# Stacking the keys and queries of the first batch pair by pair, with the expert loads behind, and two experts split early by GpSimd in place of three

## The reference, cut to what matters

```
x  = x + tanh(g_xattn) * (attention(layernorm(x), ctx) @ Wo + bo)
x  = x + tanh(g_ffn)   * moe(layernorm(x))
```

## Time and profile before

| | |
|---|---|
| median of 3 runs | 173.44 us (171.92 to 175.43) |
| the profiled execution | 172.02 us, of which its span 169.7 us |
| busy: PE, DVE, POOL, ACT | 139.7, 131.2, 126.8, 109.6 us |
| transfers | 13.99 MB, mean 82 GB/s |

### The profile page before, as it was taken

How to read it: one execution, slowest core, us unless ns; L and a number is a source line. 1 busy time by engine, 2 the same in 40 slices (tenths; PEclk the granted TensorE clock), 3 DMA queues, 4 the chain that set the end, 5 groups by cost and what they waited for, 6 DMA issues and landing times.

```text
span 169.7 us, 4332 instructions
## 1 busy us (share of the span) xinstructions
PE 139.7 (82%) x1724; PEld 111.5 (66%) x1724; DVE 131.2 (77%) x255; ACT 109.6 (65%) x182; POOL 126.8 (75%) x90
## 2 busy tenths in 40 slices
PE   7789588558699989999998892979866995999953
PEld 4435234335478768787787792869856994999952
DVE  1779999667667868768869689989999889454691
ACT  3369583329969979899968998569523462555600
POOL 7609999919999999989777955596557585868750
PEclk9999999999999999999999999999996999999999
DMA  4598699990004800995000000340000000100000
GB/s 136 184 315 211 196 238 242 220 251 14 6 0 85 198 1 16 217 233 191 4 4 0 4 0 0 108 144 6 2 0 0 4 0 4 31 0 4 0 0 31
DMA packets 12925, 13.99 MB, mean 82 GB/s; under 512 B 1470, under 2 KB 9579, under 8 KB 12907
## 3 DMA queue, kind: packets, MB, share of 16 engines
q1 hardware_dynamic: 12906, 13.73, 30.4%
HBM read 7.18 MB, written 0.26 MB: 44 GB/s over the span
## 4 chain that ended last, share of the span: by engine, by line
PE 32%; DVE 28%; POOL 10%; ACT 9%; DMA 8%; SPq 6%; issue 5%; DVEq 0%; ACTq 0%
PE banks L906 5%; DVE kab L852 5%; PE banks L908 5%; PE banks L907 5%; POOL kab L549 4%; ACT kab L642 4%; DVE v_lo L720 3%; DMA kab<-k_nat 3%; DVE nmax L735 3%; PE banks L1006 3%; PE banks L1007 3%; PE banks L987 3%; DMA ring<-in_L_ffn_w_dram 3%; SPq L425 2%; DVE gtop L763 2%
## 5 line engine op out<-in xcount | busy, mean ns | idle before, releaser
L549 POOL TENSOR_TENSOR kab<-kab 128x1024 f16<-128x1024 f32 (+1 forms) x18 | 41.1, 2283 | 17.3 <-DVE kab L852 17.3
L521 POOL TENSOR_TENSOR p_lo<-prob,p_hi 128x768 f16<-128x768 f32 x31 | 50.3, 1642 | 3.1 <-ACT p_hi L606 2.6
L642 ACT ACTIVATE kab<-banks,b1T 128x256 f32<-128x256 f32 x72 | 28.2, 478 | 24.3 <-PE banks L908 15.9
L735 DVE TENSOR_REDUCE nmax<-banks 128x1 f32<-128x768 f32 x32 | 30.5, 954 | 12.5 <-PE banks L988 12.5
L598 ACT ACTIVATE prob<-banks 128x768 f32<-128x768 f32 x32 | 25.8, 805 | 9.1 <-PE banks L1007 8.1
L906 PE MATMUL banks<-wf,kab 128*128 128x128 f16 x144 | 26.2, 224 | 5.8 <-POOL kab L549 4.5
L606 ACT ACTIVATE p_hi<-prob 128x768 f16<-128x768 f32 x32 | 27.0, 843 | 1.0
L852 DVE CAST kab<-kab 128x1024 f16<-128x1024 f32 (+1 forms) x19 | 19.5, 1031 | 9.8 <-ACT kab L642 9.8
L908 PE MATMUL banks<-wf,kab 128*128 128x128 f16 x144 | 26.2, 224 | 0.0
L907 PE MATMUL banks<-wf,kab 128*128 128x128 f16 x144 | 26.2, 224 | 0.0
L1006 PE MATMUL banks<-qab,kab 128*128 128x256 f16 x96 | 23.0, 273 | 0.7 <-DVE qab L832 0.7
(11 more groups left out here) (144 smaller groups left out, 340.3 us busy)
## 6 DMA issues: line engine op xcount, KB each, us to landing
ring<-in_L_ffn_w_dram SPq DMA_DIRECT2D x16, 256.0 KB, 4.1
kab<-k_nat SPq DMA_DIRECT2D x4, 384.0 KB, 4.4
kab<-k_nat SPq DMA_DIRECT2D x6, 192.0 KB, 4.4
kab<-k_nat SPq DMA_DIRECT2D x2, 576.0 KB, 7.2
qab<-qo SPq DMA_DIRECT2D x2, 384.0 KB, 6.2
kab<-k_nat SPq DMA_DIRECT2D x2, 288.0 KB, 7.8
prob<-in_ctx_dram SPq DMA_DIRECT2D x2, 256.0 KB, 5.4
ring<-in_L_xattn_Wk_dram SPq DMA_DIRECT2D x2, 256.0 KB, 3.9
```

Source lines behind the costliest of these rows:

```text
L521: nc.gpsimd.tensor_tensor(p_lo[:, j % 3, dst, :], prob(j, g)[:, 0:n, :], p_hi[:, j % 3, dst, :], ALU.subtract).then_inc(pl_done, 1)
L549: nc.gpsimd.tensor_tensor(hid_lo[:, k % HB, cols], hid[:, k % 2, cols], hid_hi[:, k % HB, cols], ALU.subtract).then_inc(hl_done, 1)
L642: nc.scalar.activation(hid[:, k % 2, c * T1:(c + 1) * T1], span(2 * (k % 2), HC * T1)[:, c * T1:(c + 1) * T1], ACT.Gelu, bias=b1T[:, e * H ...
L735: nc.vector.tensor_reduce(nmax[:, i, q:q + 1], span(0, KEYS), AX_X, ALU.max, negate=True).then_inc(max_done, 1)
```

## The change

`GROUPS[0]` has four groups of one pair each in place of two groups, so the keys and queries of batch 0 go out in 32 transfers in place of 16, with the same bytes. `LOAD_AFTER` puts the load of expert 1 behind pair 2 (it was behind pair 0), and the loads of 2 and 3 behind pair 3 as before. `EARLY` is 2 in place of 3: expert 2 is split by ACT and DVE in steps 17 and 18 and no longer by GpSimd, and GpSimd splits `Wo` ahead of expert 1 in place of between 1 and 2.

```diff
@@ -63,7 +63,7 @@
 BIAS_STEP = 10
-EARLY = 3
+EARLY = 2
 FSPLIT0 = 15
@@ -130,7 +130,8 @@
-GROUPS = [[(0, 1), (1, PAIRS)], [(0, 2), (2, PAIRS)]]
+GROUPS = [[(p, p + 1) for p in range(PAIRS)], [(0, 2), (2, PAIRS)]]
+LOAD_AFTER = {2: [1], 3: [2, 3]}
@@ -434,9 +435,8 @@
             for n, (p0, p1) in enumerate(GROUPS[0]):
                 stack_k(0, p0, p1)
                 stack_q(p0, p1)
-                load_f(1 + n)
-            for j in range(1 + len(GROUPS[0]), RING):
-                load_f(j)
+                for j in LOAD_AFTER.get(n, []):
+                    load_f(j)
```

## The result

| | before | changed |
|---|---|---|
| median of 20 runs each | 172.8 us | 173.47 us |
| profiled execution, span | 172.02, 169.7 us | 173.3, 171.5 us |
| mean granted clock of PE | 0.988 | 0.959 |

The ratio is 1.0089, with a 95% interval of 1.006 to 1.0119: 1.5 us slower, where 0.85 us faster was forecast. The ratio leaves out the runs in which either kernel was over 1.5% slower than its fastest, so it can't be read off the two medians. The time lies in the stated range and within 2% of before, but on the wrong side of it.

A forecast was written before the change was run, and what follows sets the result against it. PE paces the heads, with its idle ahead of 47 us to gain. +0.2 - 2.0 + 0.95 = -0.85 us gives a median of 172.6 us; own range 171.5 to 173.6, 8-in-10 range 169.9 to 175.2 us.

The forecast's parts named there:

- Landing of pair 3's keys: Ahead of head 2: keys land at 35.5 us, ACT, DVE and PE wait behind them; +0.2 us.
- Half clock behind the one long idle: PE ahead of 38.3 us: idle of about 3.8 us; half clock no term of the sum, only a rival at 0.15.
- three short idles: PE up to head 2: waits of 1.72, 1.70 and 0.39 us become one of about 3.8 us; +0.2 us.
- GpSimd's -2.0 us: Heads: PE's two waits for GpSimd's lo parts, 0.93 and 1.08 us, both go; -2.0 us.
- rival 2: PE falls to half clock behind the idle ahead of 38.3 us, losing 1.7 us: 174.3 us; chance 0.15.
- ACT's split, +0.95 us: ACT's split of expert 2 right before the gelu table load, hidden by nothing: +0.95 us.
- Rival 1: Ahead of head 2: pair 3's keys land late, 175.1 us at a landing of 38 us; chance 0.2.
- Rival 3: Faster: keys land at 34.5 us, half-clock slice at 127 to 131 us spared; 169.9 us with both; chance 0.2.
- Loads 4 to 8: Expert loads in SP's queue: load 6 waits for DVE's split in step 18, nothing is delayed; 0.
- Batch 1 keys, forecast 0: Stacks of batch 1 stand ahead of load 4 and move with the heads; 0.

The follow-up runs named there:

- the filled idle: Changed kernel with 28 products of zeros in PE's idle ahead of the second maxima of head 2; ratio 1.0017 against the kernel before.
- both long idles filled: Changed kernel with products of zeros in PE's idles, 28 ahead of head 2's second maxima and 30 ahead of the gates' transposes; ratio 0.9954 against the kernel before.

## Why the prediction was wrong

**Landing of pair 3's keys: right.** 35.7 us for 35.5, and ACT, DVE and PE behind it in the order given; +0.40 us for +0.2. SP was 0.57 us late at the load of expert 1, 0.4 us of it by one held issue (1.03 us at 27.38 us), and the landing came 6.5 us behind the load's first issue in place of 6.9. That the load in front decides it was half right: with the load moved away it landed only 0.3 us earlier, and SP's issuing is the main part.

**Half clock behind the one long idle, at nothing in the sum: this is the step that failed.** The forecast hands three short idles to one of 3.8 us for +0.2 us, and lets GpSimd's -2.0 us arrive in full behind it; half clock is rival 2 at 0.15 and no term of the sum. The idle came, 3.59 us, and half clock with it: +1.16 us in the step behind it (zero with the idle filled), and +0.29 us up to head 5, with ACT kept waiting 2.69 us in that step. GpSimd's two waits went, but 1.45 us of the gain were given back this way. Shown by the filled idle and by `EARLY` = 2 alone, where 1.86 of the 2.01 us arrive. With both long idles filled the kernel is 0.8 us faster than before, which is the forecast's sum within its interval. Rival 2 had the mechanism and nearly the price, 1.7 us. That the median lies even in the forecast's own 171.5 to 173.6 us is luck: they were reckoned from a median of 173.44 us of three runs, and twenty gave 172.8 us.

**ACT's split, +0.95 us: right**, +0.94 us measured and 1.2 us gained by moving it. What I left out is its consequence: PE's wait for the gates grew from 3.04 to 3.99 us, and half clock followed in each execution whose wait was 3.99 us and unfilled; the rest of the changed kernel took 0.3 us more than with the wait filled. I had the 3.04 us row in front of me as a case without half clock and did not ask what 0.95 us more would do. That it is the length alone is not shown: behind a wait of 2.46 us, with the split moved, the clock fell too.

**Rival 1, late keys,** did not happen: every engine stood behind the keys as it says, but they landed 0.2 us behind the forecast, and the 32 transfers in place of 16 did not make the sum this rival's. **Rival 3** did not happen: the dip near 130 us stayed. **Loads 4 to 8:** the load of expert 6 was issued at 102.86 us and nothing waited for it, as forecast.

**Batch 1 keys, forecast 0:** +0.5 us. Of the executions profiled, PE's waits for them sum to 0.80 to 0.84 us in the four with two groups in batch 0, and to 0.82 to 1.50 us in the ten with pairs; the same kernel has 0.87 and 1.13 us, and with only fillings added to the changed kernel it was 0.94 and 1.50 us. What is more is mostly a second wait of 0.18 to 0.55 us, which five of the ten have and none of the four. So it may belong to the pairs; no run separates it, and its cause is open.

Sum of the forecast, corrected by the traces: +0.40 (landing) - 2.01 + 0.15 (GpSimd) + 1.16 + 0.29 (half clock) + 0.50 (batch 1 keys, open) + 0.94 (ACT's split) + 0.37 (behind it) are the 1.8 us of span. Of the last term 0.3 us go with the filled wait.

## What to carry to other kernels

Several short idles of the busiest engine and one long idle of the same sum are not the same: here TensorE went to half clock behind the long one, and the work behind it was the next to be late. When transfers are cut into pieces to have the first ones sooner, look for who waits for the last one, and what stands behind that waiter in its queue; here an engine's reuse of a buffer took the gain, for batch 1 keys that stood ahead of the first exponential in ACT's list and were not stacked before 52 us, and ordering the keys ahead of the queries that nobody needed yet gave it back. Moving ACT's item itself behind the first exponentials was not tried. Work taken over by another engine costs its full duration if it stands right before an unhidden table load; a dozen instructions earlier it was free.

## What the runs showed of the hardware

- Behind a longer idle ahead of head 2 the step from its second maxima to those of head 3 was longer: 3.58 or 3.59 us with idles up to 0.95 us, 4.06 us with 3.24, 4.74 us with 3.59, 5.31 and 5.30 us with 4.42 and 5.65. The clock could fall when PE was already at work again: 1.2 us behind the end of the idle of 3.24 us, 1 us behind one of 2.46 us.
- Half clock did not follow the length of an idle alone. Behind those four idles, and behind each unfilled 3.99 us ahead of the gates, the granted clock fell; behind 3.04 and 3.05 us there it did not, in two kernels, and behind 2.46 us, in three, it did (0.69 to 0.78 in the lowest stretch of 4 us, 0.57 in the third kernel), in two of them with the rest of the kernel no longer for it (69.3 to 69.6 us). Behind 2.81 or 2.82 us near 128 us it fell in five executions and did not in seven. From the transposes of the gates to the end it was 64.0 to 64.4 us in eleven executions, 66.5 us in two with half clock at 128 to 136 us (0.64 and 0.50, 0.52 and 0.63), and 65.6 us with half clock at 140 to 148 us. With both long idles filled, none of the stretches was below full clock.
- SP issued 64 to 192 KB transfers between SBUF tensors at one per 0.65 us, with one held issue among the sixteen of pairs 1 and 2, so that the issues more than the bytes set their pace (the traffic at 20 to 28 us was about 200 GB/s at a DMA share of 0.85, where the two groups before had up to 269). A key transfer of 96 KB landed in 2.6 us behind other keys alone and in 3.6 us with a load of 512 KB ahead of these.
- GpSimd and DVE took turns. In eleven of the fourteen profiled executions GpSimd's first instruction on the shared expert (128x1024, 1.89 us) began ahead of DVE's lo part of a projection weight (128x512); DVE's then took 1.14 to 2.33 us and ended 0.54 to 0.55 us behind GpSimd's. In three DVE's began first or with it and took 0.68 to 0.98 us, and GpSimd's took 2.34 to 2.43 us. PE's second maxima of head 1 stood at 28.9 to 29.3 us in these three, at 30.1 to 30.7 us in nine, and at 32.7 us in the two with half clock at 20 to 24 us. So single spans of two kernels are compared by stretches between marks, not by their ends.
